# The prediction's term from the first state, accumulated ahead of U

## The reference, cut to what matters

```
pred = einsum('bhji,bhj->bhi', S, kn);  r = clip(v_t - pred, -1, 1)
S = a_t[..., None] * S;   kp  = einsum('bhd,bhde->bhe', kn, S)
S = S + b_t * kn[..., None] * (v_t - kp)[..., None, :]
o = einsum('bhji,bhj->bhi', S, q_t)
R = aR_t[..., None] * R;  kpR = einsum('bhd,bhde->bhe', kn, R)
R = R + g_t * kn[..., None] * (r - kpR)[..., None, :]
o = o + einsum('bhji,bhj->bhi', R, q_t)
```

## Time and profile before

| | |
|---|---|
| median of 3 runs | 3484.47 us (3476.64 to 3485.22) |
| profiled execution | 3481.59 us, its span 3479.8 us |
| busy: PE, PEld, DVE, ACT, POOL | 2906.5, 2571.7, 2644.2, 1948.5, 1229.9 us |
| mean granted TensorE clock | 0.889 of full |
| attention's 32 chunks | about 60 to 2570 us of the span |
| experts, then the finish | about 2669 to 3413, then to 3479.8 us |

### The profile page before, as it was taken

The page is one execution under the profiler, slowest core; times in us unless marked ns, Lnnn a source line. Parts: engine busy times, 40 slices in busy tenths (PEclk is TensorE's granted clock), DMA queues, the critical chain, the costliest instruction groups (busy, mean ns, idle before and its releaser), DMA issues. The chain is left out here.

```text
span 3479.8 us, 135741 instructions
## 1 busy us (share of the span) xinstructions
PE 2906.5 (84%) x56922; PEld 2571.7 (74%) x56922; DVE 2644.2 (76%) x6931; ACT 1948.5 (56%) x5132; POOL 1229.9 (35%) x1001
## 2 busy tenths in 40 slices
PE   4888888888888888889988888888855998889980
PEld 4888887878888887878888887888744776667760
DVE  3899988999998988998898989898952444444444
ACT  3555665665555655665555665565523555655550
POOL 3122322222222323222222322222222666666664
PEclk8998888899999889988898889898877999999995
DMA  3211111111111111111111111111147777767766
GB/s 122 78 54 41 35 38 41 38 38 42 38 35 36 40 35 40 42 38 41 39 35 35 41 35 39 43 35 36 44 154 242 116 115 113 114 108 115 115 107 210
DMA packets 193480, 240.15 MB, mean 69 GB/s; under 512 B 26738, under 2 KB 171251, under 8 KB 192115
## 3 DMA queue, kind: packets, MB, share of 16 engines
q1 hardware_dynamic: 132896, 151.22, 14.4%
q0 software_dynamic: 58368, 75.80, 13.7%
q10 hardware_dynamic: 1618, 4.46, 0.3%
HBM read 96.17 MB, written 135.20 MB: 66 GB/s over the span
## 5 line engine op out<-in xcount | busy, mean ns | idle before, releaser
L391 POOL DMA_INDIRECT table<-xrow,place_i x256 | 280.4, 1095 | 764.0 <-DVE BR L866 237.8
L1475 PE MATMUL bank<-w,route 128*128 x2560 | 370.8, 288 | 35.7 <-issue 12.2
L1105 POOL COPY inv_r<-N 32x512 f32<-32x512 f32 x128 | 136.4, 1065 | 736.5 <-DVE N L842 732.5
L1475 PEld LDWEIGHTS bank<-w,route 128*128 128x128 f32 x2560 | 311.9, 192 | 104.2 <-issue 101.2
L457 DVE TENSOR_TENSOR tri<-tri,step 128x58 f32<-128x58 f32 (+13 forms) x896 | 305.5, 341 | 30.8
L456 DVE TENSOR_TENSOR step<-tri 128x58 f32<-128x58 f32 (+13 forms) x896 | 301.7, 337 | 26.4
L1490 PE MATMUL bank<-w,seen 128*128 x640 | 215.0, 418 | 52.5 <-DVE y L1563 10.2
L1551 DVE COPY to_row<-shared 128x1 int32<-128x1 int32 x228 | 35.1, 154 | 269.1 <-DMA acc<-sh_h,to_row 43.3
L1082 POOL COPY T<-L_s 32x512 f32<-32x512 f32 x64 | 38.7, 605 | 359.5 <-DVE L_s L778 358.2
L1490 PEld LDWEIGHTS bank<-w,seen 128*128 128x128 f32 x640 | 95.8, 189 | 89.2 <-issue 83.8
L589 PE MATMUL bank<-B,kT_r 64*64 64x64 f32 x2048 | 110.4, 300 | 61.4 <-DVE S L883 61.4
(11 more groups left out here) (306 smaller groups left out, 8864.7 us busy)
## 6 DMA issues: line engine op xcount, KB each, us to landing
table<-blank SPq DMA_DIRECT2D x320, 129.0 KB
shared<-table SPq DMA_DIRECT2D x228, 129.0 KB
w<-in_wpack_dram SPq DMA_DIRECT2D x16, 1540.0 KB
xrow<-table SPq DMA_DIRECT2D x92, 129.0 KB
sum<-acc SPq DMA_DIRECT2D x16, 512.0 KB
acc<-blank SPq DMA_DIRECT2D x33, 128.0 KB, 2.6
x_rows<-y SPq DMA_DIRECT2D x64, 64.0 KB
x_res<-in_x_dram SPq DMA_DIRECT2D x64, 64.0 KB
```

What stands on the lines that cost most here:

```text
L391: nc.gpsimd.indirect_dma_start(out=table, out_offset=bass.IndirectOffsetOnAxis(ap=t.place8_i[:, k:k + 1], axis=0), in_=row[:, :], in_offse ...
L1105: ins = nc.gpsimd.tensor_copy(t.inv[1][r, :, Q * (q % 2):Q * (q % 2) + Q], t.N[r, 16:32, :])
L1475: mm = nc.tensor.matmul(ps[:, begin:begin + n], t.xT_slot[i % 3][:, P * kt:P * kt + P], weights(i, 257 * kt + begin, n), start=(kt == 0), ...
```

## The change

The state's term of PR is issued ahead of U, into PR's two banks, and the accumulation is left open. After U has been copied out, the second term is accumulated into the same banks. PR takes its two banks ahead of U in the ring. Since the end of PR is now later in program order than U although its place in the list is ahead, it no longer counts on `mm_done`; a semaphore of its own, `PR_done`, takes its place.

```diff
-    jobs += two("Z") + two("X") + two("U") + two("PR") + two("SU") + ...
+    jobs += two("Z") + two("X") + two("PR") + two("U") + two("SU") + ...
...
-                signalled += kind != "O"
+                signalled += kind not in ("O", "PR")
...
                     mm.then_inc(t.sem["mm_done"], 1)
+                PR = [begin(n, "PR0"), begin(n, "PR1")]
+                four(PR, odd_unit, [(lambda r, u: t.pq[r, 0, u, :], of(t.S))], last=False, whole=True)
                 pe.wait_ge(t.sem["B_ready"], n + 1)
                 wait_emptied(pe, t, o, n, "X0")
                 pe.wait_ge(t.sem["inv_s_ready"], n + 1)
                 crossed(n, "U", [(of(t.inv[0]), of(t.B))])
                 wait_emptied(pe, t, o, n, "U1")
-                crossed(n, "PR", [(lambda r, u: t.pq[r, 0, u, :], of(t.S)),
-                                  (lambda r, u: t.pqT[r, u, 0, :], of(t.U))])
+                for ins in four(PR, odd_unit, [(lambda r, u: t.pqT[r, u, 0, :], of(t.U))], first=False, whole=True):
+                    ins.then_inc(t.sem["PR_done"], 1)
...
-                    ps = mm(n, f"PR{h}")
+                    dve.wait_ge(t.sem["PR_done"], 2 * n + h + 1)
+                    ps = o.bank(t, n, f"PR{h}")
```

More of the change, by code:

```diff
@@ L74, in order_of_jobs @@
     jobs += [("KT", f"{g}{h}") for g in range(2) for h in range(2)] + two("q") * front + [("SG", "")]
-    jobs += two("Z") + two("X") + two("U") + two("PR") + two("SU") + two("NS") * front + two("O") + [("SD", "")]
+    jobs += two("Z") + two("X") + two("PR") + two("U") + two("SU") + two("NS") * front + two("O") + [("SD", "")]
     jobs += two("W") + two("RU") + ends + [("RK", "")] * route + [("OUT", "")] + two("V") * front
@@ L163, in alloc_shared @@
              "coef_ready", "act_diag", "pool_diag", "restart_ready", "queries_made",
-             "N_ready", "T_ready", "inv_s_ready", "inv_r_ready", "B_ready", "BR_ready", "O_begun", "O_done",
+             "N_ready", "T_ready", "inv_s_ready", "inv_r_ready", "B_ready", "BR_ready", "PR_done", "O_begun", "O_done",
              "scan_done", "log_ready", "dec_ready", "plus_made", "states_ready", "pool_link", "xf_ready",
```

## The result

The kernel with the change takes 3450.0 us (median of 6 runs, 3438.5 to 3455.7); before beside it took 3482.4 (6 runs, 3476.6 to 3487.1). The ratio is 0.9903, 95% interval 0.9885 to 0.9921: faster by about 34 us, where 65 had been forecast. The profiled execution has a span of 3448.8 us, 31 less than before. From the first N to the last, attention takes 2391.1 us where it took 2427.0, which is 35.9 less; what stands before and behind it takes 4.9 us more.

A forecast was written before the change was run, and what follows sets the result against it. DVE's own work plus its waits on PE, stretched by PE's 1.2 GHz clock, was taken as the bound. Earlier keys 55.4, part of U 13, less 3 for ACT: 65 us off 3481.6 is 3416; 8-in-10 range 3388 to 3473.

The forecast's parts named there:

- The sum: Whole kernel: 55.4 + 13 - 3 = 65 us off 3481.6, giving 3416; chance 0.58.
- 21 chunks like A and 11 like B: Keys 2.22 us earlier where the clock rose inside SU (A), 0.80 where it had risen by SU (B): 55.4 us.
- 3.70 us of 64x64 matmuls in front of the pause: Moved half plus U, unbroken on PE, raise the clock during U or the pause; second half then takes 1.16 us.
- U at full clock in part: Part of U runs after the clock's rise, saving 0 to 0.84 a chunk; 0.4 taken, 13 us in 32 chunks.
- The same clock, 0.31 a chunk: Clock unchanged: PR ends 0.31 us earlier because ACT's square no longer stands before U's copy.
- DVE's waits: Wait for PR at L860 falls from 69.8 to about 20 us, for norms at L873 from 48.4 to about 35.
- ACT's cover: ACT's exponentials behind U's copy end just before NS0 is ready, 1.17 behind NS's start; 0.1 a chunk charged, 3 us.
- The ring: New bank order: O waits for DVE's second L860, covered by NS except in the last chunk, under 1 us once.
- Rival "given back": Gain lost later in the same chunk to waits for A and PQ, 46 us: 3462; chance 0.18.
- Rival "the clock does not rise earlier": Clock at U and PR unchanged, only 32 x 0.31, 10 us, gained: 3472; chance 0.13.
- half of the chunks gain: Upper end of the forecast's own range, 3440, if only half of the chunks gain.
- Rival "slower, a later rise": Clock rise slips behind NS, NS grows by some 1.6 us, 63 us lost: 3545; chance 0.08.

The follow-up runs named there:

- e8_before_filler: The kernel before with two unread matmuls (128x256 and 128x128) in PE's pause behind U, without the change; ratio 0.9875 to before.
- e3_doubled: The changed kernel with the state's term issued twice, ahead of U and again behind U in the pause; ratio 0.9988 to before.
- e7_filler: The changed kernel with one unread 128x256 matmul in PE's pause behind U; ratio 0.9855 to before.
- e12_square: The kernel before with only ACT's square of the keys moved behind the copy of U; ratio 0.9981 to before.
- e2_ring: The kernel before with only the changed ring order and PR_done, both terms interleaved behind the wait for U's copy; ratio 0.9980 to before.
- e9_fill_N: State's term behind U, R times kplus ahead of the first projection, plus two unread matmuls in PE's wait for N; ratio 0.9943 to before.
- e1_behind: The kernel before with the state's term issued behind U, ahead of the wait for U's copy, old ring order kept; ratio 0.9827 to before.

## Why the prediction was right or wrong

- **The sum.** 65 us were forecast, 34 came. The sign and the range held, and so did the mechanism where it set in: an earlier rise of the clock. The size is off by half.
- **The step that failed: "21 chunks like A and 11 like B".** The forecast took the early rise for all 32 chunks; it came in 16. Where it came its price was right: keys 2.00 earlier than before, against (21 x 2.62 + 11 x 1.20) / 32 = 2.13 forecast with the part of U. "3.70 us of 64x64 matmuls in front of the pause" was enough in 16 chunks only, and it wasn't needed: with nothing but U in front and the pause filled (e8_before_filler) the clock was up at SU in all 32. With the pause filled in the changed kernel (e3_doubled, e7_filler) no second half stayed wholly at 1.2 GHz. The Trainium skill, "TensorE: Matmul & The Clock Gate", section "A second HAM failure mode: psum-queue depth-cycling", which I had weighed and set aside, warns of short pauses between groups of matmuls that cycle through PSUM banks. The trace agrees with it in half of the chunks and not in the other. No run settled which chunks rise early in the changed kernel: the two shown differ in no instruction. The times in its profile do sort them. Of the 11 chunks in which U started 8.46 us or more behind N, one had an early rise. Of the 20 in which it started sooner, 14 had one, and in the six that had not the clock had fallen late, 4.5 to 5.2 us behind N and not 1.7 to 3.1 (two with so late a fall did rise early). That is seen in one profile; no run tested it.
- **U at full clock in part:** right in kind, half the size. U was across a change in 15 of 32 chunks, 1.46 in the one shown; from its first record to its last it took 1.86 on average in the 16 early chunks and 2.10 in the others, 0.24 less where 0.4 was taken.
- **The same clock, 0.31 a chunk:** held, like with like. The changed kernel's 16 chunks without an early rise compare with the 20 chunks like A before, where the rise came inside SU too: PR ended at 13.66 against 14.04 and the keys started at 21.37 against 21.76, 0.38 earlier. (Against all 31 chunks before it is 0.11, because 11 of those had a rise inside PR, which the change leaves to none.) e12_square's 7 us against 10 agree, but are no larger than e2_ring's.
- **DVE's waits:** forecast 20 for PR and 35 for the norms, measured 44.4 and 45.0. That follows from the failed step: in the 16 chunks without an early rise the wait for PR is 1.0 to 2.3 us, in the 14 early ones between the first chunk and the last it is 0.9 or less.
- **ACT's cover:** right. In the first chunk shown the norms' first operation starts 1.16 behind NS, 1.17 forecast.
- **The ring:** right but for the size. O's new wait shows once, 1.5 us against "under 1 once".
- **Rival "given back":** right in four of the 15 early chunks, by the waits that it named: 1.1 us for A and 1.1 for PQ where 1.08 and 0.67 stood in chunk B. These four were 2.46 us longer than the other eleven, some 10 us. The averages hide it, since keys to next N fell from 57.06 to 56.90 and 56.70: the kernel before gave back in nine of its chunks like B. It isn't the main loss: the 16 chunks without an early rise had little to give back.
- **Rival "the clock does not rise earlier":** true of 16 chunks, which is why the result lies about half way between 3416 and 3472. The forecast's own "half of the chunks gain" was put at 3440.
- **Rival "slower, a later rise":** wrong. NS took 1.99 in all 31 chunks.

## What to carry to other kernels

When work can be moved out of a place where an engine waits, move it into another wait, not ahead of the product that the wait is for: the same 64 records were worth 0.8% more in the pause than in front of U. A gain that hangs on the clock must be counted chunk by chunk, with what the engine does around the pause, and one example of a rise is no ground for taking it everywhere. Then look at what the next wait gives back: in four of the 15 chunks with an early rise all of the gain was gone by the next N, and in e9_fill_N time at the low clock left one place and came up at another.

## What the runs showed of the hardware

- A matmul of 128x256 that nobody reads, put in a pause of PE, made a kernel faster (0.9855 against 0.9903); two of them, 128x256 and 128x128, in the kernel before gave 0.9875.
- Without a pause from X to NS, PE's small matmuls at full clock were followed by idle stretches with nothing to wait for in the profile (0.96 us in the chunk shown, 43 us in e3_doubled, 21 in e1_behind, 6 with the change, 2 in e7_filler). I take it that its instructions come too slowly there; no run tested that.
- In e9_fill_N the clock fell from 2.4 to 1.2 GHz among 32x32 matmuls: in the chunk shown at the end of Z, over which PE was busy for 2.21 of 2.50 us, and in 23 of 31 chunks inside X.
